# A decoder layer's router logits: three matmuls with 16 columns become one with 32 and one with 16, and the copy out of PSUM is split over two engines

## The reference

```
x = x + attn(layernorm(x))         # z = softmax(x W_A / 4) over the rows; a Toeplitz matrix of z times x W_V, for 16 heads; then W_O, b_O
x = x + xattn(layernorm(x), ctx)   # causal cross-attention with K, V from ctx
x = x + ffn(layernorm(x))          # 2 shared experts, and 16 routed ones of which each row uses 2
```

```
logits = flat @ router_w                       # (rows, 256) x (256, 16)
probs = softmax(logits)
weights, indices = top_k(probs, 2)
weights = weights / (weights.sum(-1) + 1e-9)
comb = sum over the two of one_hot(indices, 16) * weights
```

## Time and profile before

| what | value |
| --- | --- |
| three executions | 573.6, 574.45, 577.08 us |
| their median | 574.45 us |
| the profiled execution | 573.51 us |
| its span in the profile | 571.7 us |
| TensorE busy | 541.9 us, 95% of the span |
| VectorE busy | 426.5 us, 75% |
| ScalarE busy | 255.7 us, 45% |
| GpSimd busy | 191.8 us, 34% |

### The profile page before, as it was taken

The page is one execution under the profiler, slowest core; times in us unless marked ns, Lnnn a source line. Parts: engine busy times, 40 slices in busy tenths (PEclk is TensorE's granted clock), DMA queues, the critical chain, the costliest instruction groups (busy, mean ns, idle before and its releaser), DMA issues. The chain is left out here.

```text
span 571.7 us, 12923 instructions
## 1 busy us (share of the span) xinstructions
PE 541.9 (95%) x4716; PEld 368.2 (64%) x4716; DVE 426.5 (75%) x1107; ACT 255.7 (45%) x517; POOL 191.8 (34%) x240
## 2 busy tenths in 40 slices
PE   5787889999999999999999999999999998999997
PEld 4565557566685667766786668666866675666455
DVE  5858687868885787868886888778876776677654
ACT  4565546445354254445344445434543334332332
POOL 4215150223542144223522343234421343133123
PEclk9999999999999999999999999999999999999999
DMA  8995595795439903694449743993189125300351
GB/s 256 308 367 194 182 386 180 155 322 183 112 82 251 335 17 101 148 292 151 111 100 249 242 110 77 204 310 98 51 177 325 57 74 126 64 1 1 86 102 37
DMA packets 90734, 94.70 MB, mean 166 GB/s; under 512 B 28224, under 2 KB 76224, under 8 KB 90432
## 3 DMA queue, kind: packets, MB, share of 16 engines
q1 hardware_dynamic: 90688, 94.09, 58.1%
HBM read 75.66 MB, written 12.12 MB: 154 GB/s over the span
## 5 line engine op out<-in xcount | busy, mean ns | idle before, releaser
L694 POOL TENSOR_TENSOR mid<-gated,mid 128x512 f16<-128x512 f32 x72 | 86.6, 1202 | 214.0 <-ACT mid L880 213.9
L880 ACT ACTIVATE mid<-gated 128x512 f16<-128x512 f32 x72 | 44.9, 624 | 83.3 <-DVEq L1225 80.0
L146 PE MATMUL wide<-w_d,mid 128*128 128x256 f16 x288 | 78.5, 273 | 0.0
L148 PE MATMUL wide<-w_d,mid 128*128 128x256 f16 x288 | 78.5, 273 | 0.0
L147 PE MATMUL wide<-w_d,mid 128*128 128x256 f16 x288 | 78.5, 272 | 0.0
L1203 DVE SCALAR_TENSOR_TENSOR gated<-gated,score 128x512 f32<-128x512 f32 x72 | 49.1, 682 | 37.6 <-ACT gated L875 37.5
L146 PE MATMUL rows<-h3T,w_gu 128*128 128x512 f16 x160 | 60.7, 379 | 0.3 <-DVEq L126 0.3
L146 PE MATMUL score<-h3T,w_gu 128*128 128x512 f16 x160 | 60.7, 379 | 0.2
L147 PE MATMUL rows<-h3T,w_gu 128*128 128x512 f16 x160 | 60.6, 379 | 0.0
L148 PE MATMUL rows<-h3T,w_gu 128*128 128x512 f16 x160 | 60.6, 379 | 0.0
L148 PE MATMUL score<-h3T,w_gu 128*128 128x512 f16 x160 | 60.6, 379 | 0.0
(11 more groups left out here) (249 smaller groups left out, 1402.8 us busy)
## 6 DMA issues: line engine op xcount, KB each, us to landing
toep<-z_scratch SPq DMA_DIRECT2D x14, 2048.0 KB, 18.3
stage<-comb_scratch SPq DMA_DIRECT2D x32, 512.0 KB, 8.5
toep<-z_scratch SPq DMA_DIRECT2D x4, 1024.0 KB, 11.2
x_bo<-in_x SPq DMA_DIRECT2D x8, 512.0 KB, 11.8
x_in<-in_xr SPq DMA_DIRECT2D x7, 512.0 KB, 11.1
qT<-q_scratch SPq DMA_DIRECT2D x7, 512.0 KB, 3.9
vx<-v_scratch SPq DMA_DIRECT2D x7, 512.0 KB, 5.2
out<-x_out SPq DMA_DIRECT2D x7, 512.0 KB, 3.0
```

The source lines that it names most:

```text
L146: pe.matmul(out, stationary[0], moving[0], start=start, stop=False, **kw)
L148: return pe.matmul(out, stationary[1], moving[0], start=False, stop=stop, **kw)
L694: pool.tensor_tensor(mid_slot(j, 1, late), gate_slot(j, late), mid_slot(j, 0, late), ALU.subtract).then_inc(mid_split.sem, 1)
L880: act.activation(mid_slot(j, 0, late), gate_slot(j, late), ACT.Copy).then_inc(mid_hi.sem, 1)
```

## The change

The logits of a batch's four groups of 128 rows went to 64 columns of a bank; now they go to 128 columns, seen as [half, group, expert]. For each group and each block of the contraction one matmul multiplies h3T's high half by both halves of the weights, taken side by side as 2 x 16 columns, and writes to both parts of the bank; a second multiplies h3T's low half by the weights' high half and adds to the first part. ScalarE then copies the second part, scaled, to `logit_rest` in SBUF and counts `logit_copied` up; VectorE waits for that, and its one instruction scales the first part and adds `logit_rest`. `logit_copied` was declared before and not used.

```diff
--- before.py
+++ after.py
@@ -226,6 +226,7 @@
         x_out = sb("x_out", [P, C, E])
         h3T = sb("h3T", [P, 2, K2, S], F16)
         logit = sb("logit", [P, C, NE])
+        logit_rest = sb("logit_rest", [P, C, NE])
         top = sb("top", [P, C, 8])
         top_i = sb("top_i", [P, C, 8], U32)
         top_f = sb("top_f", [P, C, 2])
@@ -430,6 +431,10 @@
         def quarter_part(q, a):
             return quarter_bank(q).rearrange("p (a c e) -> p a c e", a=2, c=C)[:, a]
 
+        def logit_parts():
+
+            return rows.bank("logit")[:, 0:2 * C * NE].rearrange("p (a c e) -> p a c e", a=2, c=C)
+
         def backwards(row):
 
             return row.rearrange("p (c t) -> p c t", t=P)[:, :, ::-1]
@@ -913,6 +918,12 @@
                 act.wait_ge(y_stored.sem, y_stored.at(b, 0))
                 act.activation(x_out[:], x_res[:], ACT.Copy).then_inc(x_kept.sem, 1)
 
+            def copy_logit(it, b):
+
+                act.wait_ge(rows.ready.sem, rows.is_ready(it, "logit"))
+                act.activation(logit_rest[:], logit_parts()[:, 1], ACT.Copy,
+                               scale=1 / (X_H * X_W)).then_inc(logit_copied.sem, 1)
+
             def move_z(b):
 
                 act.wait_ge(score.ready.sem, score.is_ready(b, "z"))
@@ -933,6 +944,7 @@
                 if c == 6:
                     move_z(it)
                     z_powers(it)
+                    copy_logit(it, it - 2)
                 if d and m:
                     take_rest(it, it - 1, 0)
                     take_rest(it, it - 1, 1)
@@ -1037,6 +1049,8 @@
                     z_powers(it + 1)
                 elif n:
                     part_turned(it, it + 1, h1T, h1T_hi, "h1")
+                if d:
+                    copy_logit(it + 1, it - 1)
 
             part_weights(range(2))
             part_turned(-1, 0, h1T, h1T_hi, "h1")
@@ -1265,9 +1279,9 @@
             def route_top(it, b):
 
                 rows.take(dve, it, "logit")
-                dve.wait_ge(rows.ready.sem, rows.is_ready(it, "logit"))
-                dve.tensor_scalar(logit[:], rows.bank("logit")[:, 0:C * NE].rearrange("p (c e) -> p c e", c=C),
-                                  1 / (X_H * X_W), None, ALU.mult).then_inc(rows.taken.sem, 1)
+                dve.wait_ge(logit_copied.sem, logit_copied.at(b, 1))
+                dve.scalar_tensor_tensor(logit[:], logit_parts()[:, 0], 1 / (X_H * X_W), logit_rest[:], ALU.mult,
+                                         ALU.add).then_inc(rows.taken.sem, 1)
                 hold(dve, rows.taken, rows.is_taken(it, "logit"))
                 for c in range(C):
                     last = dve.max(top[:, c], logit[:, c])
@@ -1607,10 +1621,12 @@
                 rows.fill(pe, it, "logit")
                 pe.wait_ge(turned.taken.sem, turned.is_taken(it - 1, "h3.1"))
                 for q in range(C):
+                    acc = logit_parts()[:, :, q]
                     for k in range(K2):
-                        last = three_passes(pe, rows.bank("logit")[:, NE * q:NE * q + NE],
-                                            parts(h3T, k, slice(P * q, P * q + P)), parts(w_r, k, slice(None)),
-                                            start=(k == 0), stop=(k == K2 - 1))
+                        hi, lo = parts(h3T, k, slice(P * q, P * q + P))
+                        pe.matmul(acc, hi, w_r[:, :, k], start=(k == 0), stop=False, skip_group_check=True)
+                        last = pe.matmul(acc[:, 0], lo, w_r[:, 0, k], start=False, stop=(k == K2 - 1),
+                                         skip_group_check=True)
                 last.then_inc(rows.ready.sem, 1)
 
             def z_product(b):
```

## The result

The changed kernel takes **575.72 us** (median of 22 executions), the kernel before 573.52 on the same chip (22 executions): a ratio of 1.0029, with a 95% interval of 1.0018 to 1.004. That is 1.0 to 2.3 us slower, and no change by the bound of 1%. The forecast was 575.9, with 572.8 to 578.0 as its range. One execution of the changed kernel took 1590.47 us; it lies apart from all the others and is left out of the ratio (the median would be 575.65 without it).

The account below looks back on a forecast made before the run. TensorE's own stream, 95% busy, was taken as the bound; 1.1 (five ends) + 1.02 (pass 2's head) - 0.20 + 0.08 = +2.0 us on 573.51 gave 575.5, put at 575.9 between two earlier readings; range 572.8 to 578.0.

Parts of the forecast that it names:

- TensorE's gain: Router logits: 16 matmuls in 0.42 us instead of 24 in 0.61, about 0.20 us a batch.
- The rival in which the weight loads set the pace: Router matmuls: each of 64 dropped loads costs its listed 96 ns, 6.1 us gained, 567.4 us; chance 0.03.
- the two-slot matmul: Router logits: a two-piece matmul costs two slots, TensorE gains nothing, 575.9 us; inside the forecast, no chance of its own.
- ScalarE's copy: Passes 2 to 6: starts 0.02 us behind the `z_powers` read-out and takes 0.25 us, between 0.20 and 0.38.
- VectorE's wait: Ends of passes 2 to 6: VectorE starts the logits 0.96 us later, waiting for ScalarE's copy behind `z_powers`.
- The hole on TensorE: Five pass ends, before the second Toeplitz quarter: TensorE stands still 0.42 us, 0.22 later after its 0.20 gain.
- the reserve of 0.1 to 0.2 us: Second mixT block's slack before its matmul: shrinks from 0.3 to 0.4 us to this and holds.
- Pass 2's head: z_invert and all behind it come 1.02 us later, reaching TensorE at its wait for mixT; nothing covers it.
- Passes 7 and 8: At their ends, without `z_powers`: 0.20 us stays gained on TensorE in pass 8; 0.08 is lost at `finish`.
- the hop: Logits' way over ScalarE's copy to VectorE: alone adds 0.28 us at the ends of passes 7 and 8.
- the covered wait: Pass ends: the copy or `add_y` delays nothing, TensorE keeps 0.20 us in all 8 batches, 571.9 us; chance 0.11.
- VectorE could not catch up its 0.96 us: After pass ends: VectorE has no idle time, each 0.96 us reaches the end, +5.9 us, 579.4 us; chance 0.06.

Follow-up runs that it names:

- Hop only: Against the changed kernel: three matmuls per block return, ScalarE still copies half of the one logits part and VectorE adds the other; 576.42 us, ratio 1.0052.
- copy twice: Against the changed kernel: ScalarE first makes a second, useless copy of the same size into a spare tile; 577.28 us, ratio 1.0072.
- `add_y` first: Against the changed kernel: VectorE does `add_y` before the routing at the ends of passes 2 to 7; 574.78 us, ratio 1.0018.
- pass 2's head only: Against the changed kernel: ScalarE copies the logits before the z work in pass 2's head and nowhere else; 575.12 us, ratio 1.0025.
- VectorE alone: Against the changed kernel: no ScalarE copy, VectorE copies the second part to SBUF itself and then adds; 572.88 us, ratio 0.9985.

## Why the prediction was right

The mechanism was the one forecast, and the time too (575.9 forecast, 575.72 measured). That the two numbers lie within 0.2 us is partly luck: my time of before was 573.9 in effect, 0.4 too high, and my difference of 2.0 was 0.2 below the 2.2 between the medians; in the trace it was 0.7 too low. By its steps:

- **TensorE's gain**: 0.20 us forecast, 0.20 measured (0.61 to 0.41), with 0.38 us for 15 distances from start to start (407.46 to 407.84), about 25 ns for 32 columns as for 16; I had 27 for 32. The rival in which the weight loads set the pace falls with it, and so does the two-slot matmul: 16 matmuls in 0.41 us are 25.6 ns each, for either width near what one slot of 16 columns was.
- **ScalarE's copy**: starts 0.03 us after the read-out ends (408.90, 408.93; 0.02 forecast) and takes 0.22 (0.25 forecast, between 0.20 and 0.38). The rule of the Trainium skill, "ScalarE: Activation LUTs", section "What ACT_TABLE_LOAD costs", by which consecutive ACTIVATEs overlap by about 93 ns, holds between ACTIVATEs here: 0.10 us between the two copies, and 0.10 between the copy and the next one at 93.04. Behind the accumulator's read-out it does not hold, as the earlier trace rows had said, and that is the one place where the forecast needed it. (My estimate of 0.45 us by that rule was short in any case: an overlap of 0.09 in place of a start 0.02 behind is 0.11, at six places an estimated 0.7.)
- **VectorE's wait**: 0.96 forecast, 1.73 - 0.79 = 0.94 measured.
- **The hole on TensorE**: 0.42 forecast, 0.41 measured; +0.22 for each end forecast, +0.20, +0.20, +0.23 and +0.15 measured in four of five. Hop only and copy twice show that the wait sets it, and `add_y` first that it is `add_y`'s.
- **The end of pass 3** cost 1.04 instead of 0.22. Part of it is a thing I had seen and not priced: the late `add_y`. In the changed kernel it starts 2.64 us after the first logits there and 2.41 to 2.43 at the other four ends, 0.22 late; before, it was later still by comparison (1.88 against 1.47 to 1.53) and harmless. With the hole open, it adds to it: 0.64 to 0.65 us instead of 0.41, in the changed kernel both times and with the copy moved in pass 2's head only. The rest is the hole of 0.58 before mixT, which comes from a DMA issue that takes long in some executions (below). Where it took its usual time, the reserve of 0.1 to 0.2 us held, as forecast.
- **Pass 2's head**: 1.02 forecast, 0.91 on VectorE and 0.83 for the stretch. The copy was 0.03 shorter, and z_invert started 0.09 us before the group of maxima had ended (93.87 against 93.55 + 0.41), where I had let it start behind. The place was wrong too: the lateness reaches TensorE at the turning of comb, where it had waited for VectorE before the change as well, and the wait for mixT behind it stays as it was (0.54 us from the start before, 0.49 with the change).
- **Passes 7 and 8**: I kept 0.20 us for TensorE and took back 0.08; measured +0.02 and 0.00. The step that failed is "so its 0.20 us stay gained": GpSimd's split of the last middle, a releaser that I had not looked at, ended 0.05 us before TensorE's matmul started, and with the change it does so again: these 0.05 us are the handover, and there was no reserve at all. With the hop the end of pass 7 would have lost more: hop only has 59.89 there, with the merged matmuls it is 59.67.

The sum was +2.0 and the stretches give +2.68: 0.82 too little at the end of pass 3, 0.19 too much in pass 2's head, 0.14 too little in passes 7 and 8, and 0.10 too much in the other four ends. About 0.5 us of it belong to that one DMA (61.53 against 61.00 with pass 2's head only). The medians differ by 2.2 us.

Of the rivals, the covered wait is what the kernels have where the hop goes, or goes ahead of the exponential: 572.7 to 572.9, and not 571.9. The gain of 1.6 us was never fully to be had, since GpSimd's split takes it at the ends of passes 7 and 8, and pass 2's head waits for VectorE; the slow DMA of pass 4 took it once more, in all three kernels (holes of 0.20 to 0.32 before mixT). That VectorE could not catch up its 0.96 us did not happen: its idle time before x_res is 0.61 us after the change too, and no hole stands before the gates.

**What stays open**: why the first transposing DMA of pass 4 takes 1.25 us to issue in some executions and up to 1.94 in others. The executions differ already about 19 us earlier: the load of vx was issued in 0.43 to 0.80 us in the four with 1.25, and in 0.90 to 1.24 in the six others. Whether one causes the other isn't shown. Nor did any run take GpSimd's split away to see the 0.20 us come back.

## What to carry to other kernels

Work moved to a less busy engine can cost more by what is queued ahead of it there than by its own length: here a copy of 0.22 us made VectorE wait 1.13 us behind an exponential, and the same copy put ahead of it made it wait 0.24. Before a gain on the busiest engine is counted, look at each waiter near that place whose releaser ends just in time, on every engine: a gain of 0.20 us in front of a split that ended only just in time was a gain of 0.00 to the next matmul here. Once such a hole is open, a further delay in the chain before it reaches the end whole (0.12 us here, with copy twice); where it is closed, it cost nothing (0.26 us more on VectorE, with VectorE alone).

## What the runs showed of the hardware that was not expected

- The first DMA_TRANSPOSE of pass 4 was issued in 1.25 us in four profiled executions (the kernel before, hop only, pass 2's head only, `add_y` first), and in 1.91, 1.88, 1.94, 1.73, 1.87 and 1.54 in the others; the last and the first of these are the same kernel. The other 13 transposing DMAs of each execution stay between 1.23 and 1.37.
- Two ACTIVATEs of 128x64 out of PSUM overlap by 0.10 us, but one behind ACTIVATION_READ_ACCUMULATOR starts 0.02 to 0.03 us after it has ended.
- A TENSOR_REDUCE over pairs, 128x128 in and 128x64 out of PSUM, takes 0.29 us; a copy of 128x64 takes 0.23.
- Up to the first logits, executions differ by up to 2.5 us (88.7 to 91.2), as much as the whole effect of the change (2.2 by the medians, 2.7 in the trace). Only medians, or distances inside the span, can show it.
